# The convolution's input span as one 128-row matmul and two 64-row ones, with splits and sums in another order

## What is computed

```python
x = x + ffn0(conv(x) + cond_128 @ c_weight.T + bias)   # grouped convolution: 4 groups of 16 channels, 9 taps, padding 4
x = x + ffn1(agg_w @ x + agg_b)                        # a 64x64 mix per image, from a small softmax network
# ffn0: y = h @ weight.T + bias, plus a LoRA of rank 16 chosen by image
# ffn1: scores = h @ Wr.T, top 16 of 64 gates (softmax), out = ((h @ A.T) * gates) @ B * 2
```

## Time and profile before

| | us |
|---|---|
| median of 3 runs | 669.21 |
| lowest, highest | 666.76, 670.43 |
| the profiled execution | 671.31 |
| its span | 669.5 |
| TensorE busy | 651.7 (97%) |
| VectorE busy | 451.1 (67%) |
| ScalarE busy | 213.1 (32%) |
| GpSimd busy | 73.2 (11%) |

### The profile page before, as it was taken

The page is one execution under the profiler, slowest core; times in us unless marked ns, Lnnn a source line. Parts: engine busy times, 40 slices in busy tenths (PEclk is TensorE's granted clock), DMA queues, the critical chain, the costliest instruction groups (busy, mean ns, idle before and its releaser), DMA issues.

```text
span 669.5 us, 8350 instructions
## 1 busy us (share of the span) xinstructions
PE 651.7 (97%) x3197; PEld 538.4 (80%) x3197; DVE 451.1 (67%) x688; ACT 213.1 (32%) x275; POOL 73.2 (11%) x91
## 2 busy tenths in 40 slices
PE   9999999997999999999999999999899999999996
PEld 7878888886897787887789788888689888888775
DVE  2859469549377788658669648636867847656864
ACT  2714134224134115335114312334323321333510
POOL 1499200000000070000000042000000000000000
PEclk9999999998999999999999999999999999999999
DMA  8577715976968836776985682374987664047684
GB/s 306 189 293 277 288 48 160 353 218 216 381 222 317 349 148 253 261 233 234 338 305 186 273 314 94 107 225 157 348 316 266 270 258 162 0 140 206 227 318 182
DMA packets 51450, 157.98 MB, mean 236 GB/s; under 512 B 5472, under 2 KB 6368, under 8 KB 51424
## 3 DMA queue, kind: packets, MB, share of 16 engines
q1 hardware_dynamic: 46096, 148.05, 60.6%
q10 hardware_dynamic: 5328, 9.61, 4.7%
HBM read 131.94 MB, written 25.71 MB: 235 GB/s over the span
## 4 chain that ended last, share of the span: by engine, by line
PE 59%; DMA 19%; DVE 14%; issue 3%; ACT 3%; ACTq 1%; SPq 0%; DVEq 0%
PE bank L1349 14%; PE bank L1351 13%; PE bank L1350 13%; DMA gate_x<-gates 12%; PE bank L1363 8%; DMA piece_lo<-kept 4%; PE bank L1383 3%; DMA raw<-pieces 3%; DVE piece_lo L882 2%; PE bank L1370 2%; ACT piece_hi L639 2%; DVE work L977 1%; DVE x L914 1%; DMA toep<-taps 1%; PE bank L1375 1%
## 5 line engine op out<-in xcount | busy, mean ns | idle before, releaser
L882 DVE TENSOR_TENSOR piece_lo<-raw,piece_hi 128x1024 fp32r<-128x1024 f32 x60 | 74.1, 1240 | 89.9 <-ACT piece_hi L639 89.7
L1349 PE MATMUL bank<-piece_hi,u_hi 128*128 128x512 f32 x272 | 109.0, 401 | 8.1 <-DVE piece_lo L882 4.6
L639 ACT ACTIVATE piece_hi<-raw 128x1024 fp32r<-128x1024 f32 x60 | 63.3, 1057 | 155.0 <-PE bank L1351 110.6
L1350 PE MATMUL bank<-piece_lo,u_hi 128*128 128x512 f32 x272 | 107.9, 397 | 0.0
L1351 PE MATMUL bank<-piece_hi,u_lo 128*128 128x512 f32 x272 | 107.8, 396 | 0.0
L1349 PE MATMUL bank<-v_hi,piece_hi 128*128 128x512 f32 x256 | 101.8, 398 | 0.0
L1351 PE MATMUL bank<-v_hi,piece_lo 128*128 128x512 f32 x256 | 101.1, 395 | 0.0
L1350 PE MATMUL bank<-v_lo,piece_hi 128*128 128x512 f32 x256 | 101.0, 394 | 0.0
L1349 PE MATMUL bank<-piece_hi,v_hi 128*128 128x512 f32 x192 | 76.2, 397 | 1.3 <-DMA piece_lo<-kept 1.3
L1351 PE MATMUL bank<-piece_hi,v_lo 128*128 128x512 f32 x192 | 75.8, 395 | 0.0
L1350 PE MATMUL bank<-piece_lo,v_hi 128*128 128x512 f32 x192 | 75.7, 394 | 0.0
(11 more groups left out here) (143 smaller groups left out, 800.2 us busy)
## 6 DMA issues: line engine op xcount, KB each, us to landing
raw<-pieces SPq DMA_DIRECT2D x76, 512.0 KB, 5.3
piece_hi<-kept SPq DMA_DIRECT2D x48, 512.0 KB, 4.9
piece_lo<-kept SPq DMA_DIRECT2D x48, 512.0 KB, 5.8
conv_in<-conv_x SPq DMA_DIRECT2D x16, 516.0 KB, 6.9
x<-x SPq DMA_DIRECT2D x16, 512.0 KB, 5.3
gate_x<-gates ACTq DMA_DIRECT2D x32, 256.0 KB
out<-x SPq DMA_DIRECT2D x32, 256.0 KB, 4.6
conv_in<-pieces SPq DMA_DIRECT2D x12, 512.0 KB, 8.7
```

The costliest lines, as they stand in the source:

```text
L639: act.activation(piece_hi[:, n % SLOTS, :], raw[:, r % RAWS, :], ACT.Copy).then_inc(s_piece_hi, 1)
L882: dve.tensor_tensor(piece_lo[:, n % SLOTS, :], raw[:, r % RAWS, :], piece_hi[:, n % SLOTS, :].bitcast(F32), ALU.subtract).then_inc(s_piece ...
L1349: pe.matmul(to, left_hi, right_hi, start=first, stop=False)
L1350: pe.matmul(to, left_hi, right_lo, start=False, stop=False)
```

## The change

**Convolution.** Of the 256 input rows of a block, the middle 128 reach all eight output positions; the 64 rows on the left reach only the first four, the 64 on the right only the last four. `conv` becomes `conv_middle` (128 rows, 128 columns), `conv_left` (rows 64 to 127 of the array, 64 columns) and `conv_right` (rows 0 to 63, 64 columns). To put them there, the lower half of `conv_in` is stored one element later than the upper, and each load of it, and of the taps, becomes two. A left and a right matmul of different images, so of different banks, stand next to each other. `s_conv_edge` orders two sums into one bank. In the first group the edges of image b go with those of b - 1; the last right edges come within the first piece of ffn0. In a trip the order is by fours: four middles, then edges, and `s_conv` counts two images at a time.

**Order of splits and sums.** In the first group the splits of pieces 20 to 23 stand among the sums and splits of the combined weights, no longer behind them. In each trip the low part of piece 25 comes before `sums(4)`. At the end of the last trip `partial` is added to x ahead of the last product, and that product is added from its banks.

The diff, without the declarations, the new shape of `toep` and its load, and the counts of the last stores:

```diff
@@ -315,8 +322,11 @@
-                sp.dma_start(conv_in[:, 2 * t:2 * t + 2].rearrange("p b g q -> p (b g q)"),
-                             conv_x[bass.ds(g, 1), t].rearrange("a p n -> (a p) n")).then_inc(s_convin[t], 16)
+                width = 2 * CG * (Q + 1)
+                for half in range(2):
+                    at = t * width + 1 - half
+                    sp.dma_start(conv_in[half_rows(half), at:at + width],
+                                 conv_x[g, t, half_rows(half), :]).then_inc(s_convin[t], 16)
@@ -802,10 +812,14 @@
-                for step in range(4):
-                    combined_hi(2, step)
-                for n in range(20, 24):
-                    split_first(n)
+                split_first(20)
+                combined_hi(2, 0)
+                combined_hi(2, 1)
+                split_first(21)
+                combined_hi(2, 2)
+                combined_hi(2, 3)
+                split_first(22)
+                split_first(23)
@@ -1134,11 +1148,15 @@
-                combine(2)
-                for step in range(4):
-                    combined_lo(2, step)
-                for n in range(20, 23):
-                    split_first(n)
+                combine(2, 0)
+                split_first(20)
+                combine(2, 1)
+                combined_lo(2, 0)
+                combined_lo(2, 1)
+                split_first(21)
+                combined_lo(2, 2)
+                combined_lo(2, 3)
+                split_first(22)
@@ -1196,7 +1214,7 @@
-                    dve.wait_ge(s_conv, g * GB + b + 1)
+                    dve.wait_ge(s_conv, g * GB + b // 2 * 2 + 2)
@@ -1287,9 +1305,9 @@
+                split_raw(g, 25)
-                split_raw(g, 25)
@@ -1325,12 +1343,22 @@
-                for s in range(2):
-                    won(dve, g, 1, 6, s)
-                    add_partial(1 - s, s, s_o)
-                    read(s_o, 17 + 3 * s)
-                    add(partial[:, s, :], 2 + s, 0, s_o)
-                    add(partial[:, s, :], 2 + s, 1, s_o)
+                if last:
+                    for s in range(2):
+                        for h in range(2):
+                            add(partial[:, s, :], 2 + s, h, s_o)
+                    for s in range(2):
+                        won(dve, g, 1, 6, s)
+                        for h in range(2):
+                            read(s_o, 17 + 2 * s + h)
+                            add(banks[1 - s][:, :], 2 + s, h, s_o)
+                else:
+                    for s in range(2):
+                        won(dve, g, 1, 6, s)
+                        add_partial(1 - s, s, s_o)
+                        read(s_o, 17 + 3 * s)
+                        add(partial[:, s, :], 2 + s, 0, s_o)
+                        add(partial[:, s, :], 2 + s, 1, s_o)
@@ -1358,11 +1386,22 @@
-            def conv(b, bank, cg):
-                for h in range(2):
-                    mm = pe.matmul(banks[bank][:, cg * P:(cg + 1) * P], conv_in[:, b, cg, h:h + Q],
-                                   toep[:, cg, 1 - h, :], start=(h == 0), stop=(h == 1))
-                return mm
+            def conv_middle(b, bank, cg):
+                at = (b * CG + cg) * (Q + 1) + 1
+                pe.matmul(banks[bank][:, cg * P:(cg + 1) * P], conv_in[:, at:at + Q], toep[:, cg, C:3 * C],
+                          start=(cg == 0), stop=False, skip_group_check=True)
+            def conv_left(b, bank, cg):
+                at = (b * CG + cg) * (Q + 1)
+                rows = half_rows(1)
+                return pe.matmul(banks[bank][:, cg * P:cg * P + C], conv_in[rows, at:at + Q],
+                                 toep[rows, cg, 3 * C:4 * C], start=False, stop=(cg == CG - 1), skip_group_check=True)
+            def conv_right(b, bank, cg):
+                at = (b * CG + cg) * (Q + 1) + 2
+                rows = half_rows(0)
+                return pe.matmul(banks[bank][:, cg * P + C:(cg + 1) * P], conv_in[rows, at:at + Q],
+                                 toep[rows, cg, 0:C], start=False, stop=(cg == CG - 1), skip_group_check=True)
@@ -1455,6 +1494,12 @@
                     pe.wait_ge(s_piece_lo, n + 1)
+                def last_right():
+                    pe.wait_ge(s_conv_edge, GB)
+                    for cg in range(CG):
+                        mm = conv_right(GB - 1, 4 + (GB - 1) % 4, cg)
+                    mm.then_inc(s_conv, 1)
@@ -1468,6 +1513,8 @@
                             mm.then_inc(s_piece_used, 1)
+                        if n == 0 and t == 0:
+                            last_right()
                         if j == 3:
@@ -1488,14 +1535,22 @@
                     if b % 2 == 0:
-                        pe.wait_ge(s_convin[b // 2], 16)
+                        pe.wait_ge(s_convin[b // 2], 32)
                     if b >= 4:
                         if b == 0:
-                            pe.wait_ge(s_taps[cg], 16)
-                        mm = conv(b, 4 + b % 4, cg)
-                    mm.then_inc(s_conv, 1)
+                            pe.wait_ge(s_taps[cg], 32)
+                        conv_middle(b, 4 + b % 4, cg)
+                    if b:
+                        pe.wait_ge(s_conv_edge, b)
+                    for cg in range(CG):
+                        left = conv_left(b, 4 + b % 4, cg)
+                        if b:
+                            right = conv_right(b - 1, 4 + (b - 1) % 4, cg)
+                    left.then_inc(s_conv_edge, 1)
+                    if b:
+                        right.then_inc(s_conv, 1)
                     if b == 0:
@@ -1600,18 +1655,31 @@
-                for b in range(GB):
-                    if b % 2 == 0:
-                        pe.wait_ge(s_convin[b // 2], g * 16 + 16)
-                    if b == 0:
-                        pe.wait_ge(s_o, g * 22 - 12)
-                    if b == 2:
-                        pe.wait_ge(s_o, g * 22 - 8)
-                    if b >= 4:
-                        pe.wait_ge(s_item, g * ITEMS + CONV0 + b - 3)
-                    for cg in range(CG):
-                        mm = conv(b, CONV_BANKS[b], cg)
-                    mm.then_inc(s_conv, 1)
+                for four in range(0, GB, 4):
+                    for b in range(four, four + 4):
+                        if b % 2 == 0:
+                            pe.wait_ge(s_convin[b // 2], g * 32 + 32)
+                        if b == 0:
+                            pe.wait_ge(s_o, g * 22 - 12)
+                        if b == 2:
+                            pe.wait_ge(s_o, g * 22 - 8)
+                        if b >= 4:
+                            pe.wait_ge(s_item, g * ITEMS + CONV0 + b - 3)
+                        for cg in range(CG):
+                            conv_middle(b, CONV_BANKS[b], cg)
+                    for b in (four, four + 2):
+                        for cg in range(CG):
+                            left = conv_left(b, CONV_BANKS[b], cg)
+                            right = conv_right(b + 1, CONV_BANKS[b + 1], cg)
+                        left.then_inc(s_conv_edge, 1)
+                        right.then_inc(s_conv_edge, 1)
+                    for b in (four, four + 2):
+                        pe.wait_ge(s_conv_edge, g * GB + (b + 2))
+                        for cg in range(CG):
+                            left = conv_left(b + 1, CONV_BANKS[b + 1], cg)
+                            right = conv_right(b, CONV_BANKS[b], cg)
+                        left.then_inc(s_conv, 1)
+                        right.then_inc(s_conv, 1)
                 pe.wait_ge(s_o, g * 22 - 6)
```

More of the change, by code:

```diff
@@ L203, in adaln_ffn_kernel @@
         s_conv = sem("s_conv")
+        s_conv_edge = sem("s_conv_edge")
         s_lora_h = sem("s_lora_h")
@@ L544, in group @@
                     for h in range(2):
-                        store(g, 2 + t, h, 18 + 3 * t + h)
+                        store(g, 2 + t, h, 21 + 2 * t + h if last else 18 + 3 * t + h)
                 if not last:
```

13 lines of the change are left out of this document (8 added, 5 removed).

## The result

The changed kernel takes 716.81 us (median of 4 runs, 714.84 to 718.32), the kernel before beside it 669.82 (666.76 to 673.29): 1.070 times as long, 95% interval 1.064 to 1.076. The forecast of 674.0 missed by 43 us, and its range of 659 to 697 did not reach the time.

A forecast was written before the change was run, and what follows sets the result against it. TensorE, busy 97% of the span, was taken to bound the kernel. From 671.31 us, +12.0 for the loop, +4.8 for the first group and -12.0 for the reorderings gave 676.1, or 674.0 for the median; range 659 to 697.

The forecast's parts named there:

- reorderings: Splits, sums and end of the last trip in new order: waits for late weight pieces and end work go, -12.0 us.
- The pair of edges: Convolution: left and right matmul run side by side at the weight-load rate, 0.223 us a pair, saving nothing on TensorE.
- rivals B: Convolution: left and right edges run serially, 0.446 us a pair; slower, 696 us, chance 0.20.
- C: Convolution: pairs run at the streaming rate, 0.114 us, shape changes free or hidden; 664 or 660 us, chance 0.27.
- What the loop waits for: Loop's convolution: VectorE gets images later, TensorE waits for banks; 4.0 us lost per trip, 12.0 for three.
- Piece 20: First group: its low part is ready earlier, the 3.4 us wait, restart and lower clock go; 5.4 us saved.
- Piece 25: Each trip: low part moved ahead of four sums, ready 4.8 us sooner; three waits go, 5.4 us saved.
- The end: Last trip: four adds move into VectorE's wait, two per half stay behind the last product; 1.2 us less.
- Rival D: Reorderings only move the waits, half of the 10.8 us comes back; 679 us, chance 0.13.
- First group: First group's convolution: unpaired edges, shape changes and 1.2 us more wait for the softmax's exponential; +4.8 us.
- DMA. I put nothing.: Split loads of convolution input and taps: a few more 0.4 us issues on SyncE's queue, which is ahead; 0 us.
- the clock: Priced only behind piece 20's wait, where the lower clock loses 1.7 us that would be regained; no loss forecast elsewhere.

The follow-up runs named there:

- e1: Kernel before with only the new order of splits and sums and the new end of the last trip; 660.37 us, ratio 0.985.
- e9: Changed kernel with e5's whole loads, e8's order and nine matmuls of ones between the middles of image 0; 681.7 us, ratio 1.019.
- e8: Changed kernel with the split of a weight piece in each trip done behind image 3 instead of image 1; 711.78 us, ratio 1.060.
- e5: Changed kernel with each load of taps and convolution input in one transfer (other sums than the reference's); 703.64 us, one of four runs 686.26.
- e3: Kernel before with loads of taps and convolution input in two halves of 64 rows, matmuls untouched; 684.99 us, ratio 1.023.
- e7: Changed kernel with the edges streaming 32 of their 64 columns, half of their sums left out; 725.38 us, ratio 1.081.
- e4: Changed kernel with 29 matmuls of ones, 8 ahead of and 21 between the middles of image 0; 703.2 us, ratio 1.047.
- e6: Changed kernel with the four left edges of a pair of images issued before the four right ones in the trips; 727.78 us, ratio 1.085.

## Why the prediction was wrong

| part | forecast | measured | from |
|---|---|---|---|
| reorderings | -12.0 | -11.2 | e1 |
| form of the convolution, loads whole, clock full | +16.8 | +26.7 | e9 - e1 = 23.1, less 2.0 of ones, plus 5.6 (e8) |
| halved loads | 0 | +13.8 | after - e5; e3: 13.4 |
| low clock, mostly in the first group | 0 | +17.4 | the two times of e5 |
| sum | +4.8 | +46.7 | measured whole: +47.0 |

The rows aren't strictly additive (a late load also brings the clock down). That they close to 0.3 us is in part built in: 13.8 and 17.4 together are after less e5's faster execution. What stands by itself is e3's 13.4 for the loads, e9 for the form and e1. Of the 9.9 us by which the second row exceeds its forecast, 3.2 are the pause, 3.0 waits for weights from memory, 1.8 the difference between the two medians of before that are subtracted; some 2 aren't assigned.

- **The pair of edges** was right: 0.22 us, for the reason given. Its halves run side by side, and it isn't cheaper than the matmul that it replaces, so the new form had only order to lose. The trace excludes the prices of rivals B (0.446) and C (0.114), and e7 the reason of C.
- **What the loop waits for** was right in mechanism and size: 4.2 us in the third trip for 4.0 forecast. The first two lost more, 8.6 and 5.5, by the late weight piece and the lower clock. The VectorE chain, read from the earlier trace rows alone, gave 6.7, 11.6 and 18.3 us where 6.8, 11.6 and 18.4 came.
- **The reorderings** were right. Piece 20: the way from ffn0's first product to the first trip is 5.2 us shorter in e1, for 5.4 (1.0 is given back in the convolution behind it). Piece 25: 1.3, 2.5 and 1.4 us in the three trips, 5.2 for 5.4. The end: TensorE ends 9.9 us earlier and the span is 11.2 shorter, so 1.2 for 1.2. Rival D is dead: no wait took the place of those that went.
- **First group**, +4.8: at full clock (e9) 6.8 less 2.0 of ones, 4.8, with the exponential's wait at 1.5 for 1.2. Size and mechanism were right for a clock that I took to be full.
- **The step that failed is "DMA. I put nothing."** I counted bytes and looked past the issue: for the taps half the rows cost 0.65 us of queue, where all rows cost 0.72. The earlier trace rows had the warning, 0.6 us of waiting for taps, so that load was already on the path, and a cost in front of a wait that exists has no cover. The forecast also named SyncE's queue as ahead, and it is not so ahead of the first trip. Measured: 13.8 us after, 13.4 in the kernel before. Against e5's trace after is 7.1 us later at the first LoRA product and loses 6.0 more at the wait at 347.7 us and the low clock around it.
- **The second failed step is the clock.** The prediction priced the clock where a wait was removed and did not ask where a new wait would take it away: it took the convolution's clock as full. The first group's late taps took it for 47.8 us, in other runs the 2 us waits of trips two and three did; e5's two times put 17.4 us on such a loss.
- **Not foreseen:** the pause at the jump back (3.2 us) and 3 us more of waiting for weights from memory.

## What to carry to other kernels

Splitting a load in two to place its halves costs an issue per half; look for it wherever the profile already shows a wait for that tensor. A matmul with small tiles has to be priced by its weight load, and one whose load binds, as in e7, saves nothing by streaming less. Where a change adds a wait to a TensorE that runs full, price the clock behind the wait as well as the wait: in e5 17 us stood behind waits of 1.5. A wait that the list puts down to nobody, or to an engine whose work another run shows not to be needed, is to be looked up in the other engines' rows and in the queue of instructions.

## What the runs showed of the hardware

- The clock, once low, stayed low in after through 33 us of convolution without idle time (14.4 to 47.6 us) in mixed 128- and 64-row matmuls, and came back 10.2 us after its fall in e3's 128-row ones, 3.2 of these idle; e4 and e9 show the same mixture leaving a full clock full.
- This TensorE loop cost 1.3 to 1.9 us at each jump back in ten runs and nothing in seven, by its place in the program, with instruction packets in every trip in the ten and none behind the first trip in the seven. The list of waits puts it down to an innocent add.
- By the records in e6 a right matmul starts before lefts that stand ahead of it in the program. The Trainium skill, TensorE: Matmul & The Clock Gate, "Step-by-step: what each phase is for", says that only weight loads are pulled ahead and matmuls stay in program order; the records of this trace don't agree, if their lines are assigned rightly. That they are is borne out by the semaphore increments: in both lines one stands at the eighth record, where the program has it.
- Semaphore increments in a row on TensorE took 4.9 to 5.0 us for each 32 between 32, 64 and 96 of them, 0.15 us each; the first 32 showed only 1.0 us, perhaps because TensorE still had matmuls in flight, which no run tests.
